# Four parts of a two-layer network in one kernel: barriers between them removed, steps of neighbouring parts interleaved by a table

## The reference, cut to what matters

```python
for layer 0:
    x = x + xattn0(layernorm(x), ctx)      # 8 heads, keys and queries scaled to length 1, softmax over columns
    x = x + ffn0(layernorm(x))             # 256 -> 1024, gelu twice, 1024 -> 256, both products with ternary weights
for layer 1:
    x = x + xattn1(layernorm(x), ctx)      # 16 query heads on 4 key heads, 128 wide, rms norm, rotary positions
    x = x + ffn1(layernorm(x))             # 256 -> 2 x 704, silu(gate) * up, 704 -> 256, ternary weights
```

## Time and profile before

| stage (us from the start) | length | PE | DVE | ACT | POOL | clock |
|---|---|---|---|---|---|---|
| opening, 0 to 169 | 169.0 | 123.2 | 118.7 | 117.7 | 94.9 | 0.90 to 0.92 |
| first feed-forward until its first Gelu, 169 to 179.6 | 10.6 | 4.2 | 9.9 | 1.2 | 4.4 | 0.50 |
| its Gelus, 179.6 to 232.2 | 52.6 | 36.6 | 46.7 | 51.5 | 32.6 | 0.98 |
| its end, 232.2 to 242.5 | 10.3 | 5.8 | 4.7 | 0.0 | 2.8 | 0.70 |
| attention, filling, 242.5 to 282.2 | 39.7 | 22.7 | 23.3 | 23.1 | 28.7 | 0.86 |
| attention, steady, 282.2 to 679.3 | 397.1 | 389.6 | 376.3 | 378.2 | 316.9 | 1.00 |
| attention, emptying, 679.3 to 711.4 | 32.1 | 24.9 | 19.7 | 19.1 | 5.9 | 0.95 |
| last feed-forward until its first Silu, 711.4 to 721.4 | 10.0 | 3.6 | 8.4 | 3.4 | 4.0 | 0.66 |
| its Silus, 721.4 to 775.6 | 54.2 | 41.5 | 52.4 | 29.3 | 25.9 | 0.97 |
| its end, 775.6 to 791.7 | 16.1 | 9.7 | 8.3 | 1.7 | 5.1 | 0.61 |

### The profile page before, as it was taken

One profiled execution on the slowest core, in us unless ns is written; L12 is line 12 of the kernel. 1 busy time (PEld: TensorE's weight loads), 2 busy tenths in 40 slices (PEclk: granted clock), 3 DMA queues, 4 the chain that ended last, 5 costly groups with the idle time before them and its releaser, 6 DMA issues. The chain is left out here.

```text
span 791.7 us, 16306 instructions
## 1 busy us (share of the span) xinstructions
PE 661.8 (84%) x4660; PEld 387.7 (49%) x4660; DVE 668.3 (84%) x1668; ACT 625.3 (79%) x2103; POOL 521.1 (66%) x705
## 2 busy tenths in 40 slices
PE   2688788846755689999999999999999999875776
PEld 0233333312333356666666666666666666542443
DVE  4889758568972799999999999999999999858995
ACT  2578878739972799999999999999999999835551
POOL 4666665335753887787887788778878887503553
PEclk9989989669995999999999999999999999998996
DMA  7556766402451469878878886797788879730445
GB/s 287 147 156 166 207 166 200 126 7 56 92 101 20 94 121 163 138 134 141 145 138 129 151 147 135 127 155 139 133 147 140 138 129 162 139 59 17 81 95 129
DMA packets 308521, 102.05 MB, mean 129 GB/s; under 512 B 285392, under 2 KB 303952, under 8 KB 308176
## 3 DMA queue, kind: packets, MB, share of 16 engines
q1 hardware_dynamic: 308432, 101.02, 63.4%
HBM read 22.33 MB, written 8.39 MB: 39 GB/s over the span
## 5 line engine op out<-in xcount | busy, mean ns | idle before, releaser
L1232 ACT ACTIVATE psum<-psum,arena 128x256 f32<-128x256 f32 x256 | 136.0, 531 | 19.7 <-DVE arena L1348 19.7
L1304 DVE SCALAR_TENSOR_TENSOR arena<-psum,arena 128x256 f16<-128x256 f32 x256 | 111.0, 475 | 0.5 <-ACT arena L1249 0.5
L1249 ACT ACTIVATE arena<-psum,arena 128x256 f16<-128x256 f32 x256 | 100.6, 476 | 4.1 <-DVE arena L1317 1.2
L1394 PE MATMUL psum<-wq_t,arena 128*128 128x512 f16 x384 | 94.6, 383 | 10.2 <-DMA arena<-arena 6.7
L1186 POOL TENSOR_TENSOR arena<-arena 128x512 f32<-128x512 f32 x64 | 81.4, 1271 | 31.2 <-DVE arena L1323 31.1
L1426 PE MATMUL psum<-arena 128*128 128x512 f16 x384 | 93.6, 379 | 5.4 <-DVE arena L1331 5.4
L1438 PE MATMUL psum<-wo_t,arena 128*128 128x256 f16 x768 | 95.5, 275 | 0.1
L1416 PE MATMUL psum<-arena 128*128 128x256 f16 x768 | 94.3, 273 | 1.2 <-DMA arena<-arena 1.0
L825 ACT ACTIVATE arena<-psum 128x1024 f32<-128x1024 f32 x64 | 65.7, 1029 | 27.6 <-PE psum L981 27.5
L1438 PEld LDWEIGHTS psum<-wo_t,arena 128*128 128x128 f16 x768 | 75.4, 98 | 23.2 <-DVE arena L1331 0.4
L1323 DVE TENSOR_TENSOR arena<-psum,arena 128x1024 f32<-128x1024 f32 x64 | 78.4, 1225 | 6.6 <-PE psum L1394 6.6
(11 more groups left out here) (169 smaller groups left out, 1597.9 us busy)
## 6 DMA issues: line engine op xcount, KB each, us to landing
split_scratch<-arena SPq DMA_DIRECT2D x48, 128.0 KB, 2.0
arena<-split_scratch SPq DMA_DIRECT2D x32, 192.0 KB, 4.0
arena<-arena SPq DMA_TRANSPOSE x272, 3.3
arena<-in_ctx SPq DMA_DIRECT2D x16, 256.0 KB, 3.6
x_rows<-in_x SPq DMA_DIRECT2D x4, 512.0 KB, 9.3
arena<-in_b_w SPq DMA_DIRECT2D x2, 1024.0 KB, 8.6
arena<-in_wq SPq DMA_DIRECT2D x4, 512.0 KB, 5.7
arena<-in_wo SPq DMA_DIRECT2D x4, 512.0 KB, 5.5
```

Source lines behind the costliest of these rows:

```text
L1232: last = eng.activation(s_banks(u)[:, h, :], s_banks(u)[:, h, :], ACT.Exp, bias=bias[:, u % 2, h:h + 1], scale=r_q(u)[:, h:h + 1], accum_o ...
L1249: hi = eng.activation(p_hl[:, u % 2, 0, h, :], s_banks(u)[:, h, :], ACT.Copy, scale=share[:, u % 2, h:h + 1])
L1304: last = eng.scalar_tensor_tensor(p_hl[:, u % 2, 1, h, :], s_banks(u)[:, h, :], share[:, u % 2, h:h + 1], p_hl[:, u % 2, 0, h, :], ALU.mul ...
L1394: mm = eng.matmul(Q_BANK, y_t[:, b % 2, x, k, :], c.wq_t[:, w, k, SHARE * P * g:SHARE * P * g + SHARE * P], start=(n == 0), stop=(n == 5))
```

## The change

1. There is one barrier, at the end. Each part's function for an engine becomes a generator that yields ahead of every step, and one table says in which order all five engines take the steps:

```diff
+ORDER = (("a", 76), ("b", 2), ("a", 3), ("b", 1), ("a", 3), ("b", 1), ("a", 3), ("b", 1), ("a", 2), ("b", 8),
...
+         ("c", 58), ("d", 2), ("c", 2), ("d", 1), ("c", 1), ("d", 1), ("c", 1), ("d", 1), ("c", 1), ("d", 1),
...
+            for name, count in ORDER:
+                for _ in range(count):
+                    next(engines[name], None)
...
+            barrier(eng)
```

2. In place of the barriers stand waits on what a part needs of the one before. The first takes the tile it starts on, the next two the banks or buffers that the part before used:

```diff
@@ part_ffn, vector
             if t is not None:
+                eng.wait_ge(given, each * (t + 1))
                 eng.bn_stats(stats[:, t % 2, :], c.x_rows[:, t, :]).then_inc(S["stats"], 1)
@@ part_ffn, tensor, at the first wide and the first narrow projection
+                if t == 0:
+                    eng.wait_ge(*first_wide)
...
+                if t == 0:
+                    eng.wait_ge(*first_down)
@@ part_c, sync, ahead of the first turn of probabilities
+                if u == 0:
+                    eng.wait_ge(ffn["q2"], BATCHES)
+                    eng.wait_ge(ffn["mx2"], BATCHES)
+                    eng.wait_ge(ffn["ss2"], BATCHES)
@@ part_c, scalar, at the first probabilities
+                if u == 0:
+                    eng.wait_ge(ffn["act"], BATCHES)
@@ part_c, vector, statistics of a batch
+                eng.wait_ge(ffn["out"], b + 1)
@@ part_c, tensor, at the first scores and the first attended unit
+                if u == 0:
+                    eng.wait_ge(ffn["gelu"], BATCHES)
...
+                if u == 0:
+                    eng.wait_ge(ffn["out"], BATCHES)
@@ program
+        b = part_ffn(core, "b", core.ternary["b1"], None, core.ternary["b2"], None, (70, 79), (0, 34), core.opened, 2, (core.opened, 2 * BATCHES), (core.opened, 2 * BATCHES))
+        d = part_ffn(core, "d", core.ternary["d2"], core.ternary["d1"], core.ternary["d3"], out, (23, 33), (40, 64),
+                     core.attended, 1, (core.spent, 128), (core.attended, BATCHES))
```

```diff
+    EARLY = 2
@@ part_c, pool
+            b = batch(s, ROWS)
+            if b is not None and b < 2:
+                eng.wait_ge(S["stats"], 3 * (b + 1))
+                wait(eng, S["y"], b)
+                eng.tensor_tensor(rstd[:, :], var[:, :], c.minus_half[:, 0:1], ALU.pow).then_inc(S["rstd"], 2)
...
+                if u < EARLY:
+                    eng.wait_ge(S["r"], 2 * u + 1)
+                    eng.tensor_tensor(r[:, u % 8, :], log_ms[:, :], c.minus_half[:, 0:6], ALU.pow).then_inc(S["r"], 1)
@@ part_c, scalar
+            if s == PROJ + EARLY:
+                eng.preload_act_table_set("natural_log_exp_and_others")
@@ part_c, vector
+                if u < EARLY:
+                    eng.wait_ge(S["ss_q"], u + 1)
+                    eng.wait_ge(S["ss_k"], u + 1)
+                    wait(eng, S["r"], 2 * u)
+                    eng.tensor_scalar(log_ms[:, :], sums[:, u % 2, :], 1.0 / HEAD_DIM, 1e-6 * W_SCALE * W_SCALE,
+                                      ALU.mult, ALU.add).then_inc(S["r"], 1)
...
+                eng.wait_ge(S["stats"], 3 * b + 2)
+                eng.tensor_scalar(var[:, :], mv[:, 1:2], LN_EPS, None, ALU.add).then_inc(S["stats"], 1)
```

More of the change, by code:

```diff
@@ L29 @@
 LN_EPS = 1e-5
-ARENA = 20 * 1024
+ARENA = 23 * 1024
 ROUND = 1.5 * 2.0**23
@@ L70, in local, with region @@
         return got
-    def new_part(self):
-        self.used = 0
+    def region(self, first, last):
+        self.used, self.limit = 256 * first, 256 * last
     def sem(self, name):
@@ L135, in ffn_signals, with part_ffn @@
     return S, turned1, turned2, c.sem("ffn_kept")
-def part_ffn(core, name, up, gate, down, x_dram):
+def part_ffn(core, name, up, gate, down, x_dram, early, late, given, each, first_wide, first_down):
     c = core
@@ L152, in part_ffn @@
     SLOTS = 6
-    yc = c.local("yc_" + name, [P, 2, D])
+    c.region(*late)
     act1 = c.local("act1_" + name, [P, 2, WIDE])
@@ L1057, in tensor_weights @@
         return step
+    c.opened = S["added"]
     return sync, pool, scalar, vector, tensor
@@ L1066, in part_c @@
     c = core
+    ffn = c.ffn_signals[0]
     GROUPS = KV_HEADS
@@ L1270, in scalar @@
                 eng.activation(v[:, u % 8, 0, :, :], kv_view[:, :, 1, :], ACT.Copy).then_inc(S["v_hi"], 1)
+            if u is not None and u >= EARLY:
                 eng.wait_ge(S["ss_q"], u + 1)
@@ L1273, in scalar @@
                 wait(eng, S["r"], 2 * u)
-                eng.activation(log_ms[:, :], sums[:, u % 2, :], ACT.Ln, scale=1.0 / HEAD_DIM, bias=eps[:, 1:2])\
+                eng.activation(log_ms[:, :], sums[:, u % 2, :], ACT.Ln, scale=1.0 / HEAD_DIM, bias=eps[:, :])\
                    .then_inc(S["r"], 1)
             b = batch(s, ROWS)
-            if b is not None:
-                eng.wait_ge(S["stats"], 2 * (b + 1))
+            if b is not None and b >= 2:
+                eng.wait_ge(S["stats"], 3 * (b + 1))
                 wait(eng, S["rstd"], 2 * b)
-                eng.activation(log_var[:, :], mv[:, 1:2], ACT.Ln, bias=eps[:, 0:1]).then_inc(S["rstd"], 1)
+                eng.activation(var[:, :], var[:, :], ACT.Ln).then_inc(S["rstd"], 1)
                 eng.wait_ge(S["rstd"], 2 * b + 1)
                 wait(eng, S["y"], b)
-                eng.activation(rstd[:, :], log_var[:, :], ACT.Exp, scale=-0.5).then_inc(S["rstd"], 1)
+                eng.activation(rstd[:, :], var[:, :], ACT.Exp, scale=-0.5).then_inc(S["rstd"], 1)
             score = unit(s, SCORE)
@@ L1289, in scalar @@
             u = unit(s, PROJ)
-            if u is not None:
+            if u is not None and u >= EARLY:
                 eng.wait_ge(S["r"], 2 * u + 1)
@@ L1449, in program, with steps @@
         constants_pool = constants(core)
-        makers = (
-            lambda: opening(core, x, ctx_in, [("b1", b_w1, 1024, D), ("b2", b_w2, D, 1024), ("d1", d_w1, 704, D),
-                                              ("d2", d_w2, 704, D), ("d3", d_w3, D, 704)], (wq, wkv, wo),
-                            (positions, rows)),
-            lambda: part_ffn(core, "b", core.ternary["b1"], None, core.ternary["b2"], None),
-            lambda: part_c(core),
-            lambda: part_ffn(core, "d", core.ternary["d2"], core.ternary["d1"], core.ternary["d3"], out),
-        )
-        parts = []
-        for n, make in enumerate(makers):
-            core.new_part()
-            parts.append((make(), end_part(core, n)))
-        block = ctx.enter_context(nc.Block())
+        a = opening(core, x, ctx_in, [("b1", b_w1, 1024, D), ("b2", b_w2, D, 1024), ("d1", d_w1, 704, D),
+                                      ("d2", d_w2, 704, D), ("d3", d_w3, D, 704)], (wq, wkv, wo),
+                    (positions, rows))
+        b = part_ffn(core, "b", core.ternary["b1"], None, core.ternary["b2"], None, (70, 79), (0, 34), core.opened, 2, (core.opened, 2 * BATCHES), (core.opened, 2 * BATCHES))
+        c = part_c(core)
+        d = part_ffn(core, "d", core.ternary["d2"], core.ternary["d1"], core.ternary["d3"], out, (23, 33), (40, 64),
+                     core.attended, 1, (core.spent, 128), (core.attended, BATCHES))
+        parts = {"a": a, "b": b, "c": c, "d": d}
+        barrier = end_part(core, 0)
+        block = ctx.enter_context(nc.Block())
+        def steps(eng, n):
+            engines = {name: part[n](eng) for name, part in parts.items()}
+            for name, count in ORDER:
+                for _ in range(count):
+                    next(engines[name], None)
+            for engine in engines.values():
+                for _ in engine:
+                    raise AssertionError("steps left over")
+            barrier(eng)
         @block.sync
         def _(eng):
-            for (sync, _, _, _, _), barrier in parts:
-                sync(eng)
-                barrier(eng)
+            steps(eng, 0)
         @block.gpsimd
@@ L1472, in _ @@
             constants_pool(eng)
-            for (_, pool, _, _, _), barrier in parts:
-                pool(eng)
-                barrier(eng)
+            steps(eng, 1)
         @block.scalar
         def _(eng):
-            for (_, _, scalar, _, _), barrier in parts:
-                scalar(eng)
-                barrier(eng)
+            steps(eng, 2)
         @block.vector
@@ L1485, in _ @@
             eng.wait_ge(core.consts_ready, 6)
-            for (_, _, _, vector, _), barrier in parts:
-                vector(eng)
-                barrier(eng)
+            steps(eng, 3)
         @block.tensor
         def _(eng):
-            for (_, _, _, _, tensor), barrier in parts:
-                tensor(eng)
-                barrier(eng)
+            steps(eng, 4)
 def laid_out(inputs):
```

54 lines of the change are left out of this document (37 added, 17 removed), and 3 rows, old and new, of the table ORDER.

## The result

The changed kernel took 785.84 us (median of 20 runs, 778.0 to 792.4) beside 792.25 for the kernel before (20 runs, 787.5 to 794.5): ratio 0.991, 95% interval 0.989 to 0.993. It is faster by 0.9%, where 1.5% was forecast (779.4). The changed kernel's runs spread along with the mean granted TensorE clock, from 778.0 at 0.964 to 792.4 at 0.937. The medians differ by 6.4, but the profiled execution took 789.65, 3.8 above its median, and its span of 787.9 is only 3.8 shorter than that of before.

The account below looks back on a forecast made before the run. Inside a stage one engine or pair is full, so time is lost at the seams: 19.5 saved at the first two, less 1.5 lock, 2.8 variance row and 3.0 third seam, is 12.2; 791.6 becomes 779.4 us, range 765 to 788.

Parts of the forecast that it names:

- First seam: Opening to first feed-forward: first Gelu moves from 179.65 to 175.0 with the table load hidden, 4.6 us saved.
- Second seam: First feed-forward interleaved with the attention's start: 19.5 us saved by the first and second seams together, ends 12 to 26.
- price of C4: Early attention step on VectorE amid the first feed-forward: 6.45 us with its waits, POOL's six-column power taken as 1.0.
- From C6 to C9 the old kernel took 19.7: Attention's start in the second seam: 19.7 us before becomes 23.3 with feed-forward rows among its steps, ending at 262.7.
- VectorE must issue it in order: Early attention step in the second seam: VectorE waits in it for ScalarE and POOL while feed-forward rows queue behind.
- Lock: Two-input VectorE rows of the first feed-forward stretched beside POOL's rows: 24 times at most 0.23 us, 1.5 lost.
- Variance row: Steady attention: added VectorE row for the variance's small addend costs 0.2 us a batch, 14 times, 2.8 lost.
- Third seam: Attention's end interleaved with the last feed-forward: fills make an attention step 2.5 late, then lockstep; 3.0 us lost, ends 0 and 6.
- If TensorE stays fast: Third seam: projection to product takes 4.1 us instead of 5.0, and the loss is 0.3.
- Hollow overlap: Rival: added waits hold the parts apart as the barriers did, only the first seam gains; about 789 us, chance 0.08.
- The waits hide: Rival: early attention and last feed-forward steps find their partners done; 766 us, chance 0.25 for below 772.
- Longer attention steps: Rival, and sign of a wrong forecast: attention steps grow; 0.21 us more each eats the gain, 0.3 gives 797; chance 0.07.

Follow-up runs that it names:

- e6: Changed kernel plus spare TensorE matmuls in the second seam, and the logarithm's bias back for batches 2 to 15 without the VectorE row; 781.28 us, ratio 0.984.
- e3: Changed kernel with the variance's addend in batches 2 to 15 again a bias of ScalarE's logarithm, without the added VectorE row; 777.06 us, ratio 0.980.
- e10: Changed kernel with the last feed-forward's first four steps left in place and its later ones behind the attention's last step; 780.19 us, ratio 0.985.
- e7: Changed kernel with all first feed-forward steps ahead of the attention's first, without a barrier; 796.57 us, ratio 1.007 to the kernel before.
- e4: Changed kernel with all last feed-forward steps behind the attention's last, without a barrier; 786.37 us, ratio 0.993 to the kernel before.
- e13: Changed kernel with logarithm bias back, second-seam spare matmuls, POOL's fills early, most last feed-forward steps behind the attention, and VectorE's fill wait later; 774.26 us, ratio 0.980.
- twin: The changed kernel run again without any edit, on the same chip as three other kernels; 786.62 us, ratio 0.987 to the kernel before.

## Why the prediction was right, and where it was off

The direction and the range held (785.84 in 765 to 788, 0.991 in place of 0.985), but only about half of the forecast saving came, and six of the twenty runs lie above 788, the profiled one among them: that the median falls inside owes something to the width of the range. In the profiled execution 3.8 of the forecast 12.2 are left. The 8.4 between come apart into: TensorE's clock 6.2 (112.1 less e6's 105.9, of which some 0.3 is e6's missing VectorE row in C8), the shared lock and what is left of the second seam 3.1, the variance row and C48 1.6, the first seam 0.1 and the end 0.1; against that the third seam 0.9 better and 1.8 from the opening, which the forecast had not changed.

- *First seam, 4.6.* Right: 4.5, with the table load hidden and the projection as the last wait.
- *Second seam.* The price of C4 (6.45; 6.6 from 216.30 to B17's first row at 222.88) was right, though POOL's power on six columns took 1.33 and not the estimated 1.0. **The step that failed** is "From C6 to C9 the old kernel took 19.7", from which came the 23.3: it kept the old kernel's TensorE durations, in a stretch whose granted clock had been 1.00, for a TensorE that now comes out of waits of 2.6 to 4.5 us. It measured 28.8 in one execution, and 24.6 to 24.7 in the five kernels with spare matmuls; from C6 to C11 VectorE waited 7.9 for TensorE. The prediction held the means to see it: it charged just this for the third seam, by the earlier trace rows, and not for the second. So C9 started at 269.5 and not near 263. The sum's "VectorE must issue it in order" was followed to VectorE's queue but not to TensorE's, where L452 waits for L361.
- *Lock, 1.5.* Mis-sized: nine of the 24 rows met a POOL row and cost 3.6, all fifteen rows above 5.6. The 0.23 a row was taken from one meeting; here a VectorE row was stretched by up to 0.62, beside a POOL row of 1.12. The Trainium skill, "SBUF — State Buffer", section "SBUF: two separate sides", has the lock last a whole instruction; the trace agrees, in that all fifteen rows end within 0.03 of a POOL row. The upper end of 5.5 was the better guess. That it is the lock which costs 3 us was read from the ends of rows; no run took POOL's rows away.
- *Variance row, 2.8.* 4.4 in the trace, of which e3 took back 3.7: 0.28 for each of the 13 batches between C11 and C66 rather than 0.2, since the next step's first row is pushed too.
- *Third seam, 3.0 lost.* Right in sign and parts: 2.3 in C67, turns of 8.8 and 8.3, together 2.1 lost from C66 to D7. The prediction's "If TensorE stays fast" came true in e3: at a clock of 0.97 the seam, 58.7, is no longer a loss against 60.4. e10 shows the other way out: without the lockstep the seam gives 3.9, at a clock of 0.89.
- *Rivals.* "Hollow overlap" is refuted by e7. "The waits hide" did not happen: VectorE's waits in C4 and C5 are 3.2 and 3.3. Longer attention steps did not come either, but for the variance row and C48.

## What to carry to other kernels

Look past a barrier to the chain behind it: without barriers but in the old order, e7's second seam was slower than with one, and e4's third seam only 1.4 faster. When steps of two parts are interleaved, follow each engine's queue for what it now waits behind, TensorE's too, and price its work after such a wait at the clock that a like gap shows in the trace. Bring forward the steps that prepare data, and leave in one piece those in which every engine hands over to the next; a wait that is moved earlier is only gone if its partner got there earlier as well.

## What was not expected of the hardware

The clock after a gap is not fixed by the code: the same instructions of the second seam took 108.9 to 112.3 in six executions, at clocks of 0.90 to 0.83. The opening varies too: in ten of the thirteen kernels, all with one opening, the first Gelu started between 172.5 and 173.9, but at 175.2 in e7, 169.4 in e10 and 166.8 in e13. The granted clock from the start to the first Gelu was 0.88 to 0.90 in the ten, 0.92 in e10 and 0.95 in e13; e7's 0.885 does not explain its start. Stretch view of 150 to 160, first the changed kernel at a granted clock of 0.51, then e13 at 0.98, by then some us further on in the program:

```profile
150.00:160.00 10.00, 9.73 (x76) 3.21 (x69) 4.34 (x13) 5.26 (x7) 1.39 (x5) 0.51 0.01 2
```

```profile
150.00:160.00 10.00, 6.08 (x68) 2.78 (x66) 6.59 (x23) 8.33 (x7) 2.59 (x7) 0.98 0.00 0
```

So the same code varies by some us (the twin's six runs lay between 776.7 and 790.9), and a small edit here is better judged by the length of its stretch than by one time.
